# One PSUM bank moved from the ring of the row maxima to the ring of projections and transpositions

## The reference

```
x = layernorm(tgt, ln1);  q, k, v = heads(x @ sa_wqkv)
wei = softmax(causal(q @ k^T) * scale);     result = tgt + merge(wei @ v) @ sa_wproj + b
xq = layernorm(result, ln2);  xs = layernorm(src, ln2)
k2, v2 = heads(xs @ ed_wkv);  q2 = heads(xq @ ed_wq)
wei2 = softmax(q2 @ k2^T * scale);          result = result + merge(wei2 @ v2) @ ed_wproj + b
result = result + relu(layernorm(tgt, ln3) @ ff_w1 + b1) @ ff_w2 + b2
```

## Time and profile before

| | |
|---|---|
| median of 3 runs | 644.02 us (643.61 to 646.34) |
| the profiled execution's own time | 644.92 us |
| its span in the trace | 643.0 us |
| TensorE matmul busy | 559.7 us, 87% |
| VectorE busy | 415.2 us, 65% |
| ScalarE busy | 325.0 us, 51% |
| GpSimd busy | 129.5 us, 20% |
| mean granted TensorE clock | 0.959 of 2.4 GHz |

### The profile page before, as it was taken

How to read it: one execution, slowest core, us unless ns; L and a number is a source line. 1 busy time by engine, 2 the same in 40 slices (tenths; PEclk the granted TensorE clock), 3 DMA queues, 4 the chain that set the end, 5 groups by cost and what they waited for, 6 DMA issues and landing times.

```text
span 643.0 us, 14141 instructions
## 1 busy us (share of the span) xinstructions
PE 559.7 (87%) x5564; PEld 452.3 (70%) x5564; DVE 415.2 (65%) x982; ACT 325.0 (51%) x613; POOL 129.5 (20%) x370
## 2 busy tenths in 40 slices
PE   3497887898989999898899999999899998987796
PEld 3395676776877777777777777767677777766564
DVE  5984474788557656698448657697457645584371
ACT  2142553446635655456635655366535656374064
POOL 6701321113003212022003112031013011130010
PEclk9966997999999999999999999999999999999799
DMA  8296029296671048293580067392740166006600
GB/s 240 71 134 129 1 69 128 56 110 72 114 122 52 11 89 129 61 127 61 120 135 6 23 97 125 69 123 65 121 85 1 35 107 123 2 10 108 87 2 15
DMA packets 73122, 52.08 MB, mean 81 GB/s; under 512 B 21920, under 2 KB 72288, under 8 KB 73056
## 3 DMA queue, kind: packets, MB, share of 16 engines
q1 hardware_dynamic: 73056, 51.17, 48.5%
HBM read 14.36 MB, written 1.84 MB: 25 GB/s over the span
## 4 chain that ended last, share of the span: by engine, by line
PE 44%; DVE 22%; SPq 14%; ACT 7%; DMA 6%; issue 5%; POOL 1%; DVEq 0%; POOLq 0%; ACTq 0%
SPq L538 14%; PE misc L1074 9%; DVE negm L843 7%; DMA k2st<-kp 5%; PE pvb L1045 5%; PE misc L931 4%; PE mxb L1013 4%; PE scb L1029 4%; PE misc L932 3%; PE misc L933 3%; PE misc L1081 3%; DVE rem L777 3%; ACT prob L714 2%; ACT kp L699 1%; DVE stats L753 1%
## 5 line engine op out<-in xcount | busy, mean ns | idle before, releaser
L714 ACT ACTIVATE prob<-scb 125x448 f32<-125x448 f32 (+1 forms) x256 | 134.1, 543 | 69.8 <-PE scb L1029 66.0
L843 DVE TENSOR_REDUCE negm<-mxb 112x1 f32<-112x375 f32 x256 | 128.9, 540 | 25.8 <-PE mxb L1013 24.0
L1013 PE MATMUL mxb<-k2st,q2st 96*112 96x375 bf16 x256 | 82.5, 338 | 2.5 <-DVE negm L843 1.9
L633 POOL CAST mparts<-negm 112x8 bf16<-112x8 f32 x64 | 12.3, 191 | 332.4 <-DVE negm L843 165.0
L1029 PE MATMUL scb<-q2st,k2st 128*125 128x112 bf16 x768 | 74.6, 223 | 4.9 <-ACT prob L714 4.2
L1029 PEld LDWEIGHTS scb<-q2st,k2st 128*125 128x125 bf16 x768 | 64.7, 137 | 17.7 <-ACT prob L714 9.7
L840 DVE TENSOR_REDUCE negm<-mxb 112x4 f32<-112x448 f32 x64 | 39.6, 619 | 51.2 <-PE mxb L1010 51.1
L1045 PE MATMUL pvb<-prob,v 125*17 125x112 f32 (+1 forms) x2048 | 65.0, 261 | 0.1
L1074 PE MATMUL misc<-wf,hT 128*112 128x256 f32 x256 | 63.0, 396 | 1.0 <-DVE rem L777 1.0
L1074 PEld LDWEIGHTS misc<-wf,hT 128*112 128x112 f32 x256 | 46.8, 186 | 12.6 <-DVE rem L777 2.2
L1045 PEld LDWEIGHTS pvb<-prob,v 125*17 125x17 f32 (+1 forms) x2048 | 44.2, 97 | 15.2 <-issue 11.4
(11 more groups left out here) (153 smaller groups left out, 1246.4 us busy)
## 6 DMA issues: line engine op xcount, KB each, us to landing
k2st<-kp SPq DMA_DIRECT2D x192, 93.8 KB, 4.5
xs<-in_ctx SPq DMA_DIRECT2D x16, 375.0 KB
q1st<-qp SPq DMA_DIRECT2D x48, 112.0 KB, 5.6
k1st<-kp SPq DMA_DIRECT2D x48, 112.0 KB, 6.9
q2st<-qp SPq DMA_DIRECT2D x96, 56.0 KB, 2.3
xn<-in_x SPq DMA_DIRECT2D x4, 448.0 KB, 5.7
tb<-in_x SPq DMA_DIRECT2D x8, 224.0 KB, 9.5
out<-ostage SPq DMA_DIRECT2D x16, 112.0 KB, 3.4
```

The source lines that it names most:

```text
L714: nc.scalar.activation(prob[0:rows, n % PROB_SLOTS, :], scb[n % SCORE_BANKS][0:rows, 0:GH * T], ACT.Exp, scale=SCALE).then_inc(s_ex, 1)
L843: V.tensor_reduce(negm[:, at, i:i + 1], mx[0:T, 0:S], axis=AX_X, op=ALU.max, negate=True).then_inc(s_mx, 1)
L1013: mm = M(mx[0:T, 0:S], q2st[0:NROW, i, b * T:(b + 1) * T], k2st[k2_place(q, b)][0:NROW, i, 0:S], start=True, stop=True)
```

## The change

One line. The ring `misc` gets three banks in place of two, the ring `mxb` two in place of three.

```
@@ -46,7 +46,7 @@
 SLOTS = 6
 K_PART = (0, 1, 2, 0, 1, 0)
 Q_PART = (0, 0, 0, 1, 1, 2)
-MISC_BANKS, MAX_BANKS, SCORE_BANKS = 2, 3, 2
+MISC_BANKS, MAX_BANKS, SCORE_BANKS = 3, 2, 2
 PROB_SLOTS = 6
 FF2_PIECES = 2
 LEAD = 4
```

## The result

The changed kernel takes 650.5 us (median of 8 runs, 649.88 to 653.54) against 647.04 us for the kernel before on the same chip: ratio 1.0062, 95% interval 1.0034 to 1.0091. It is slower, by about 4 us; I had forecast no change (643.1 us, range 638.0 to 648.5). Of the 7.4 us between 643.1 and 650.5, 3.0 are the kernel before: its median came out at 647.04 over 8 runs, and I had worked from 644.02 over 3. On 644.02 the ratio gives 648.0. In the profiled executions the span went from 643.0 to 648.0 us and the mean granted clock from 0.959 to 0.950.

What follows compares the result with a forecast made beforehand. No engine alone was the bound: it changes hands inside a group's 141.6 us. Gains of 12.1 us on `misc` less losses of 11.2 on `mxb` gave -0.9 us, the median from 644.02 to 643.1, range 638.0 to 648.5.

Steps and rivals of the forecast that it cites:

- the item "319.8 us": First `v2` runs inside the wait for the second `k2`'s reader: 1.15 us a group, three groups, 0.3 in the last.
- the gains: Waits of TensorE on ring `misc` saved by its third bank: 12.1 us in sum, ends 6 and 15.
- the clock that hung on it: Behind 319.8 us, slow clock might not come with less idle time: 0 to 3.0 us less 0.6, taken as 1.2.
- unit 5's loss: VectorE's stretch, 283 to 293 us: a late `max` leaves VectorE dry; 1.0 us a group, 3.1 us in all.
- Two signs: Forecast wrong if the clock falls at other places behind new waits, or a group's period isn't within 1.5 us of 141.6.
- The losses: Ring `mxb` with two banks: 3.1 us at 283 to 293, 6.6 at 329 to 343, 1.5 in last group; 11.2.
- The gains outside 319.8: `misc` waits saved: period start 3.9 us, 248 us 1.6, 259 to 273 us 1.2, prologue 0.4.
- the period start: 216 to 226 us: waits of `k2` and `sT` go; 1.0 us a group, four times, 3.9 in all.
- the items to 273 us: Waits at 248 us and at 259 to 273 us shortened: 0.4 us a group each, 1.6 and 1.2 in all.
- the prologue: Third `qk1` waits 2.24 us for `rem`; VectorE, nearly full there, gains its two holes, 0.4 us.
- the second: Rival: slower by unit 7's first `max`, if `v2` misses the 319.8 wait and the clock stays down; 648 to 650, 21%.
- The rule of the Trainium skill: By it two banks do for the maxima and losses are nil; rival in full 631.9, 5%, half 637.5 to 640, 22%.

Runs made afterwards that it cites:

- the own buffer: First part of a group's last `k2` put in a buffer of its own, needing no landing: 1.0006 on the changed kernel, 0.9811 on the kernel before.
- two_two: Changed kernel with two banks for each of the rings `misc` and `mxb`, one bank unused: 1.0252 of the kernel before.
- o3_early: Changed kernel with `o3` of unit 0 and its statistics one quarter earlier: 1.0222 of the kernel before.
- kp_after: Changed kernel with the first part of a group's last `k2` in a buffer of its own: 1.0006 of the kernel before.
- v2_first: Changed kernel with the two `v2` steps of the third batch ahead of the second `k2`: 1.0047 of the kernel before.
- the lent bank: Changed kernel, third `misc` bank lent to the maxima in unit 5, in units 6 to 7, or both: 1.0013, 0.9961, 0.9892 of the kernel before.
- shared_u57: Changed kernel with its third `misc` bank lent to the maxima in both stretches, unit 5 and units 6 to 7: 0.9892 of the kernel before.
- kp_tb_before: Kernel before with the last `k2`'s first part in its own buffer, and `o3` of unit 5 and `tb`'s load a quarter earlier: 0.9870.
- kp_before: Kernel before with the first part of a group's last `k2` in a buffer of its own: 0.9811.
- u57_v2: `shared_u57` with the two `v2` steps of the third batch ahead of the second `k2`: 0.9874 of the kernel before.
- u57_v2_src: `u57_v2` with the 375 KB load of the next source rows moved behind `tb`'s transfer: 0.9660 of the kernel before, 623.48 us.
- kp_tb_after: `kp_after` with `o3` of unit 5 and the load of `tb` one quarter earlier: 1.0040 of the kernel before.

## Why the prediction was wrong

The step that failed is the item "319.8 us" of the gains with the clock that hung on it, 3.8 + 1.2 of 12.1 us, and in it above all the clock. In the prediction's words: "With the idle time shorter by a `v2` the fall may or may not come: 0 to 3.0 us less the 0.6 counted above, I take 1.2." The idle time in front of the release got longer, not shorter, and what the clock took grew.

After minus before in us, by stretch of the three groups that have one behind them, in the profiled execution of each kernel:

| stretch | forecast, a group | first | second | third |
|---|---|---|---|---|
| first score of unit 2 to first of unit 4 | -0.8 | +0.24 | -1.32 | -0.98 |
| to the first `q2` | +1.0 | +1.18 | +1.18 | +2.57 |
| to the first score of unit 1 | -1.15, and the clock | +1.24 | +0.68 | -1.09 |
| to the first score of unit 2 of the next group | +1.2 | +1.16 | +1.20 | +1.20 |

The third row is where the sum went wrong: +0.8 us for the three groups, in place of 3 x -1.15 and -1.2, -4.65. It splits into three parts:

| part | first | second | third |
|---|---|---|---|
| first `q2` to ScalarE's part, which releases the bank | +0.38 | +0.03 | -0.32 |
| from there to the second `v2` | -0.80 | -1.10 | -0.79 |
| from there to the first score of unit 1 | +1.66 | +1.75 | +0.02 |

- The release. It stands 22.9 us behind the first `q2` in the first two groups before and 23.2 and 23.0 after, since a row of 24 DMAs lies between. So it moves with `q2`; its being 1.14 us later in the second group is unit 5's loss, which I had counted, and not a second one.
- The order of the steps. The second `v2` now comes 0.8 to 1.1 us sooner behind the release. I had written 1.15, and 0.3 more with the slow clock in the second group: 2.7 us in place of 3.75 in sum. The mechanism was right and the size was not: the second `v2` starts 0.65 us behind `o2` (320.94, 321.59), where I had put 0.3.
- The clock. What TensorE gained between `q2` and the second `k2` (1.5 us in the second group) couldn't move the release; it made the idle piece in front of it longer: 2.55, 2.26 and 2.93 us after, where before there were 1.53, 1.60 and 2.55. Busy time of TensorE times the missing share of the clock, summed over the windows from the release to unit 1's first score, is 0, 1.7 and 1.7 us before and 1.7, 3.2 and 1.7 us after. That is 3.2 us more, where I had taken 1.2 less, and it is nearly all of the third part's 3.4.

How sure is the step from the idle piece to the clock? The traces of all runs have 60 such places, three in each profiled execution. In the 36 of the runs with the own buffer or with `v2` first, where TensorE waits at most 1.04 us for `rem`, the clock never falls between the release and unit 1's first score. In the 24 of the other kernels, where it waits 1.47 to 4.24 us, it falls in 21: in 17 of 18 with three misc banks, in 4 of 6 with two. The falls that take 2.6 to 3.2 us in place of 1.7 come only with three banks, six times. So with the wait gone the falls at this place are gone too; that its greater length is why the changed kernel has more of them rests on these counts. Length alone doesn't settle it: in `two_two` there is a fall behind 1.47 us, in `o3_early` none behind 2.36. And a fall can move: in `kp_after` and `v2_first` it comes behind the stall at unit 7 instead.

At the first group's wait for stacks, 102 to 106 us, the gain ahead of a release is lost too: the changed kernel ends the `k2` there 2.6 us early and starts the `v2` behind the wait 0.7 us early (105.84 against 106.53). There the clock gives something back, since it is at full speed again from 109 us on and not from 112: by the next score the changed kernel is 1.8 us early.

Two signs that I had named as those of a wrong forecast came: the clock fell at a new place, in the first group, and a group's period is 143.3 us, 1.7 above 141.6. In the third group the clock also fell behind unit 5's maxima (1.7 us of its +2.57), where it hadn't before.

The losses were right within the noise: 3.1 and 6.6 us forecast, 3.2 and 6.5 measured by the lent bank, each with some 2.7 us of uncertainty, and the last row of the table is as forecast. The gains outside 319.8, 7.1 us, agree with the 7.0 (2.3 either way) of `shared_u57`. By the traces single items differ: the period start and the items to 273 us give 1.2 and 1.3 us in the second group and not my 1.0 and 0.8, the prologue 0.3 and not 0.4. That 11.2 - 7.1 = 4.1 us comes so near the measured 4.0 is luck in part: it takes the item at 319.8 as nothing, where it was a gain of 2.7 and a loss of 3.4.

Of the rivals the second came nearest, with 21%: it named this place, a clock that stays down, and 648 to 650 us. I kept it low because the order of the steps said that `v2` would get in. It did; the clock stayed down all the same, which the rival had tied to `v2` not getting in. The rule of the Trainium skill that I had weighed (Perfetto Trace Analysis, section Matmuls: rotate through banks so that evacuation and matmul overlap) doesn't give a number of banks; here the difference between two and three for the maxima is 11 us, because single reductions stand behind other work of their engine.

Three things stay open. With two misc banks the third maxima bank is worth 16 us, with three 11, and I did not find where the 5 us between come from. `kp_tb_before` is slower than `kp_before` (0.9870, 0.9811), as if the earlier `o3` and `tb` cost something; that wasn't followed. And what decides whether the clock falls behind a wait of 1.5 to 2.4 us isn't known, nor how much of the 3.2 us of clock is the luck of one profiled execution. What the change did to the last group, 0.3 us between its first score of unit 2 and the end, wasn't split.

## What to carry to other kernels

Time won in front of a release that DMA sets is worth nothing until that release moves: walk from the release back to its first cause (here the first `q2`, 23 us ahead), and count only what moves that cause, and what gets done inside the wait. What is won between the two lengthens the wait, and a longer wait can cost clock behind it: give that term a loss side too, and not only the hope of a gain. When a gain is seen in the trace of a change and isn't in the time, look for the next transfer in the same queue: here moving one large load behind a small urgent one, together with a bank lent by place and the order of `v2`, gave 3.4%, and with the own buffer in place of the order of `v2` 3.8%, many times what the split of the banks moved. How much of that the load alone gives on the kernel before wasn't measured; on `u57_v2` it gave 2.1%.

## What the runs showed of the hardware

A `DMA_DIRECT2D` issue that takes 0.35 us took 3.33 us on SyncE when it stood 1.4 us behind the issue of a 375 KB transfer with 12 stack DMAs just ahead of that, and held what was behind it on the queue: `tb` was issued 3.37 us behind its start, and 0.39 us behind it in `u57_v2_src`. In `kp_tb_after`, where the output came directly behind the 375 KB issue, it took 4.4 to 5.3 us in the three groups.

A fall of the granted clock at the place of 319.8 that came once cost TensorE's busy time 1.6 to 1.7 us. Neither the length of the idle piece nor the way in which it is cut settles whether it comes: 1.53 us with 0.28 a little behind it had none in the kernel before (first group, 1.00), 1.47 us with 0.28 behind it had one in `two_two`, and 2.36 us had none in `o3_early`. Timeline of TensorE and a window of `two_two`:

```profile
324.92 0.38 PE L931 MATMUL misc<-wv_hi,xsT_hi 128*125 128x256 f32 x1 [1.47 <-DVE rem L777]
...
326.37 0.54 PE L931 MATMUL misc<-wv_hi,xsT_hi 128*125 128x256 f32 x1 [0.28 <-ACT v L693]
...
327.00:328.00 1.00, 1.00 (x6) 0.99 (x6) 0.00 (x0) 0.00 (x0) 0.00 (x0) 0.50 0.96 131
```
